# Query and key chunks with their own loads of x and their own dates, in an attention and expert kernel

## The reference

```python
qkv = x @ Wqkv
q, k, v = jnp.split(qkv, 3, axis=-1)
...
for i in range(H):
    ...
    q_rot = _apply_rotary(q[:, i], cos, sin)
    k_rot = _apply_rotary(k[:, i], cos, sin)
    att = jnp.einsum('btd,bsd->bts', q_rot, k_rot) * scale
    if cascade_bias is not None:
        att = att + cascade_w[i - 1] * cascade_bias
    att = jnp.where(causal, -jnp.inf, att)
    att = jax.nn.softmax(att, axis=-1)
    out_i = jnp.einsum('bts,bsd->btd', att, v[:, i])
    head_outputs.append(out_i)
    cascade_bias = jnp.mean(att, axis=1, keepdims=True)
...
x = _layernorm(x + _L0_attn_ref(x, ...), axis=-1)
x = _layernorm(x + _L0_ffn_ref(x, ...), axis=-1)
```

## Time and profile before

| | us |
|---|---|
| median of 3 runs | 3427.57 |
| lowest and highest of them | 3421.42, 3430.92 |
| span of the profiled execution | 3421.5 |
| first exponential of turn 0 | 46.5 |
| first exponential of turns 8, 64, 224, 248 | 163.1, 811.3, 2798.0, 3100.3 |
| mean granted TensorE clock | 0.967 |

### The profile page before, as it was taken

One profiled execution on the slowest core, in us unless ns is written; L12 is line 12 of the kernel. 1 busy time (PEld: TensorE's weight loads), 2 busy tenths in 40 slices (PEclk: granted clock), 3 DMA queues, 4 the chain that ended last, 5 costly groups with the idle time before them and its releaser, 6 DMA issues.

```text
span 3421.5 us, 95130 instructions
## 1 busy us (share of the span) xinstructions
PE 3079.1 (90%) x29668; PEld 1592.4 (47%) x29668; DVE 2747.6 (80%) x9925; ACT 3055.5 (89%) x8882; POOL 2127.2 (62%) x6194
## 2 busy tenths in 40 slices
PE   7898888888999899999999989999999988989855
PEld 3444444443544445554554434555455544544544
DVE  7777777777888788888988897888888987888754
ACT  4999999999989989999999998999999999989634
POOL 6556566564655467876666666777766645666245
PEclk8999999999999999999999999999999999999976
DMA  5322223223334324444433423444334433444354
GB/s 164 94 79 87 85 59 87 76 73 90 93 101 111 104 84 120 120 123 131 128 111 112 123 64 110 116 120 145 104 111 117 125 83 100 130 118 136 97 185 126
DMA packets 270810, 371.12 MB, mean 108 GB/s; under 512 B 61669, under 2 KB 177389, under 8 KB 270304
## 3 DMA queue, kind: packets, MB, share of 16 engines
q1 hardware_dynamic: 255056, 326.65, 33.2%
q0 software_dynamic: 14976, 37.34, 3.8%
q10 hardware_dynamic: 272, 1.05, 0.1%
HBM read 260.02 MB, written 104.40 MB: 107 GB/s over the span
## 4 chain that ended last, share of the span: by engine, by line
PE 36%; DVE 8%; issue 7%; ACT 5%; POOL 4%; SPq 2%; DMA 1%; another core or an unknown queue 1%; POOLq 0%; DVEq 0%; ACTq 0%
PE pv L1240 8%; PE scores L1209 7%; PE scores L1222 6%; DVE att_a L1527 4%; PE side L1369 3%; PE side L1269 2%; ACT att_t L1406 2%; ACT att_a L1396 2%; PE side L1295 2%; PE side L1376 1%; PE scores L1224 1%; PE side L1283 1%; PE scores L1369 1%; SPq L2028 1%
## 5 line engine op out<-in xcount | busy, mean ns | idle before, releaser
L1396 ACT ACTIVATE att_a<-att_a,neg_max 128x128 f32<-128x128 f32 (+7 forms) x2048 | 1609.8, 786 | 52.5 <-DVE neg_max L1527 48.7
L1406 ACT ACTIVATE att_t<-scores 128x1024 f32<-128x1024 f32 (+7 forms) x2048 | 1343.0, 656 | 68.7 <-PE scores L1224 53.7
L1527 DVE CUSTOM_DVE_ANT_0 att_a<-scores,window 128x512 f32<-128x512 f32 (+3 forms) x2048 | 1146.8, 585 | 240.2 <-PE scores L1209 133.7
L1209 PE MATMUL scores<-k_stack,q_stack 99*128 99x512 bf16 (+3 forms) x3072 | 919.0, 335 | 132.6 <-DVE neg_max L1527 112.1
L1240 PE MATMUL pv<-att_t,v_sb 128*32 128x256 f32 (+7 forms) x16384 | 898.8, 299 | 1.9 <-ACT att_t L1406 1.7
L1222 PE MATMUL scores<-q_stack,k_stack 104*128 104x512 bf16 (+3 forms) x3072 | 842.7, 332 | 62.8 <-ACT att_t L1406 50.2
L1527 DVE CUSTOM_DVE_ANT_0 att_a<-scores,window,neg_max 128x512 f32<-128x512 f32 (+3 forms) x1024 | 557.8, 545 | 110.4 <-PE scores L1209 92.9
L1209 PEld LDWEIGHTS scores<-k_stack,q_stack 99*128 99x128 bf16 x3072 | 280.1, 98 | 572.8 <-DVE neg_max L1527 345.6
L1240 PEld LDWEIGHTS pv<-att_t,v_sb 128*32 128x32 f32 x16384 | 340.0, 108 | 413.0 <-issue 334.1
L1222 PEld LDWEIGHTS scores<-q_stack,k_stack 104*128 104x128 bf16 x3072 | 275.3, 98 | 402.4 <-issue 197.9
L1224 PE MATMUL scores<-identb,mask 128*128 128x128 bf16 x2048 | 451.9, 222 | 0.0
(11 more groups left out here) (307 smaller groups left out, 4367.5 us busy)
## 6 DMA issues: line engine op xcount, KB each, us to landing
runner_r<-in_experts SPq DMA_DIRECT2D x137, 384.0 KB
qk_parts<-of_proj SPq DMA_DIRECT2D x128, 384.0 KB
of_proj<-in_xt SPq DMA_DIRECT2D x29, 1024.0 KB
q_stack<-qk_parts SPq DMA_DIRECT2D x256, 96.0 KB
k_stack<-qk_parts SPq DMA_DIRECT2D x256, 96.0 KB
q_stack<-qk_parts SPq DMA_DIRECT2D x256, 64.0 KB
k_stack<-qk_parts SPq DMA_DIRECT2D x256, 64.0 KB
head_out<-o_sb SPq DMA_DIRECT2D x252, 64.0 KB
```

The source lines that it names most:

```text
L1209: engine.matmul(piece_room(c), qs[0:ROWS_A, i * P:(i + 1) * P], ks[0:ROWS_A, low:high], start=True, stop=True).then_inc(s_a_filled, 1)
L1396: engine.activation(taken, taken, EXP, scale=-1.0, bias=neg_max[:, n, i:i + 1], accum_out=row_sum[:, n, i:i + 1]).then_inc(s_exp_a, 1)
L1406: engine.activation(att_t[:, ring:ring + end - base], scores[:, base:end], EXP, accum_out=col_sum[:, n, j:j + 1]).then_inc(s_exp_b, 1)
L1527: engine.tensor_tensor_reduce(out=att_a[:, ring + low:ring + high], in0=piece_room(c), in1=window[:, T - A_LONG[p] + low:T - A_LONG[p] + h ...
```

## The change

Chunks get loads of their own, and so do values from m = 4 on: 60 loads of x instead of 32, listed in LOADS with their room. The chunks of rounds 1 to 3 begin evenly over turns 3 to 63, about five turns an m; those of rounds 4 to 7 over turns 64 to 223, ten turns an m, in four of them one each. The value jobs begin where they did. The gate product goes with the chunks. Until m = 11 the values' x lies in runner_r, all other x in of_proj. A load is put into play four turns before the job that wants it. g_keep now also waits in the plan for the readers of the routing logits two groups back, and the first tile's gather for the last reader of runner_r.

```diff
-    def x_room(m):
-        return (m % 2, m // 2 + 1) if m < SLOTS else (0, m - 1)
-    def x_before(m):
-        return m - 2 if m <= SLOTS else m - 1
     FIRST = 4 * SLOTS
+    AHEAD = 3
+    BEHIND = 3
+    def qk_turn_of(m):
+        k = m - SLOTS
+        if k < AHEAD * SLOTS:
+            return BEHIND + k * (2 * SPAN - BEHIND) // (AHEAD * SLOTS)
+        k -= AHEAD * SLOTS
+        return 2 * SPAN + k * (ROUNDS - 3) * SPAN // ((ROUNDS - 1 - AHEAD) * SLOTS)
+    def chunk_turn(n):
+        m, c = divmod(n, 4)
+        return qk_turn_of(m) + (c if m < (AHEAD + 1) * SLOTS else (0, 1, 3, 4)[c])
+    def value_turn(n):
+        m, c = divmod(n, 2)
+        r, slot = divmod(m, SLOTS)
+        return (r - 1) * SPAN + (BEHIND if r == 1 else 0) + 7 * slot + 4 + c
+    def has_room(m):
+        return m < 3 * SLOTS
+    LOADS = [(m % 2, m, "both", 0) for m in range(SLOTS)]
+    LOADS += sorted([(0, m, "qk", qk_turn_of(m)) for m in range(SLOTS, ROUNDS * SLOTS)] +
+                    [(1 if has_room(m) else 0, m, "v", value_turn(2 * m)) for m in range(SLOTS, ROUNDS * SLOTS)],
+                    key=lambda load: (load[3], load[2], load[1]))
+    LOAD_OF = {(what, m): i for i, (_, m, whats, _) in enumerate(LOADS)
+               for what in (("qk", "v") if whats == "both" else (whats,))}
+    def x_room(i):
+        return LOADS[i][0], len([k for k in range(i + 1) if LOADS[k][0] == LOADS[i][0]])
+    def x_before(i):
+        was = [k for k in range(i) if LOADS[k][0] == LOADS[i][0]]
+        return was[-1] if was else None
...
-        return [Stage("g_x", m, hold=1.5, after=(("x_load", m), ("w_center", 0))), Stage("g_turn", m, frees=True), Stage("g_keep", m)]
+        return [Stage("g_x", m, hold=1.5, after=(("x_load", LOAD_OF["qk", m]), ("w_center", 0))), Stage("g_turn", m, frees=True),
+                Stage("g_keep", m, after=tuple(("f_logit", (m // SLOTS // KT - 2) * QUADS + q) for q in range(QUADS)))]
...
-        def x_stage(m):
-            was = x_before(m)
-            gated = (("g_x", was),) if was >= 0 and with_gate(was) else ()
-            return Stage("x_load", m, after=(("v_b", 2 * was + 1), ("qk_b", 4 * was + 3)) + gated if was >= 0 else ())
+        def x_stage(i):
+            was = x_before(i)
+            if was is None:
+                return Stage("x_load", i)
+            _, m, whats, _ = LOADS[was]
+            free = (("v_b", 2 * m + 1),) if whats != "qk" else ()
+            if whats != "v":
+                free += (("qk_b", 4 * m + 3),) + ((("g_x", m),) if with_gate(m) else ())
+            return Stage("x_load", i, after=free)
...
-                if x_ == BEHIND:
-                    project(1, 0)
-                if in_round == 28 and r + 2 < ROUNDS:
-                    project(r + 2, 0)
-                if r + 1 < ROUNDS:
-                    slot, piece = divmod(in_round - (BEHIND if r == 0 else 0), 7)
-                    if 0 <= slot < SLOTS:
-                        m = (r + 1) * SLOTS + slot
-                        if piece == 6 and slot + 1 < SLOTS:
-                            project(r + 1, slot + 1)
-                        if piece < 4:
-                            begin(chunk_job(4 * m + piece), 0)
-                        elif piece < 6:
-                            begin(value_job(2 * m + piece - 4), 0)
-                        if piece == 5 and with_gate(m):
-                            begin(gate_job(m), 0)
+                for i, (_, m, _, wanted) in enumerate(LOADS):
+                    if m >= SLOTS and max(BEHIND, wanted - 4) == x_:
+                        project(i)
+                for n in range(FIRST, 4 * SLOTS * ROUNDS):
+                    if chunk_turn(n) == x_:
+                        begin(chunk_job(n), 0)
+                        if n % 4 == 3 and with_gate(n // 4):
+                            begin(gate_job(n // 4), 0)
+                for n in range(2 * SLOTS, 2 * SLOTS * ROUNDS):
+                    if value_turn(n) == x_:
+                        begin(value_job(n), 0)
...
-            r, slot = divmod(n, SLOTS)
+            r, slot = divmod(LOADS[n][1], SLOTS)
             k, was = x_room(n)[0], x_before(n)
-            if was >= 0:
-                line.wait_ge(s["v_b"], nth["v_b", 2 * was + 1])
-                line.wait_ge(s["qk_b"], nth["qk_b", 4 * was + 3])
-                if with_gate(was):
-                    line.wait_ge(s["g_x"], nth["g_x", was])
+            if was is not None:
+                _, m, whats, _ = LOADS[was]
+                if whats != "qk":
+                    line.wait_ge(s["v_b"], nth["v_b", 2 * m + 1])
+                if whats != "v":
+                    line.wait_ge(s["qk_b"], nth["qk_b", 4 * m + 3])
+                    if with_gate(m):
+                        line.wait_ge(s["g_x"], nth["g_x", m])
...
+                        if n == (0, 0):
+                            last = max(m for room, m, whats, _ in LOADS if room == 1)
+                            pool.wait_ge(s["v_b"], nth["v_b", 2 * last + 1])
```

More of the change, by code:

```diff
@@ L800, in turn @@
                     for slot in range(SLOTS):
[L801 removed]
+                        project(slot)
                         if slot == 0:
@@ L1268, in tensor_program @@
                         col = c // 2 * C + half * P
-                        made = engine.matmul(room, w_qkv[:, k, col:col + P], xT[x_room(m)[0]][:, k, c % 2 * WB:(c % 2 + 1) * WB],
+                        made = engine.matmul(room, w_qkv[:, k, col:col + P], xT[x_room(load)[0]][:, k, c % 2 * WB:(c % 2 + 1) * WB],
                                              start=(k == 0), stop=(k == KT - 1))
@@ L1282, in tensor_program @@
                                 t0 = (4 * quad + j) * P
-                                made = engine.matmul(room[:, j * P:(j + 1) * P], xT[x_room(m)[0]][:, k, t0:t0 + P],
+                                made = engine.matmul(room[:, j * P:(j + 1) * P], xT[x_room(load)[0]][:, k, t0:t0 + P],
                                                      w_qkv[:, k, col:col + P], start=(k == 0), stop=(k == KT - 1))
```

29 lines of the change are left out of this document (15 added, 14 removed).

## The result

The changed kernel takes 3456.8 us (median of 4; 3452.9 to 3462.7), the kernel before beside it 3428.5: a ratio of 1.0087, 95% interval 1.0071 to 1.0104. It is slower by 28 us where 8 us faster was forecast, and outside the range of 3395 to 3444. The late stage, at 2007 us on the profile, lies beyond every case of the prediction: the highest of them had it at 1983.

A forecast was written before the change was run, and what follows sets the result against it. ScalarE was taken to end last in turns 8 to 63, with stalls behind TensorE and VectorE side work later. Terms -13, +7, +2 and -4 for the clock gave -8 us from 3427.6: 3420 us, range 3395 to 3444.

The forecast's parts named there:

- the highest of them: Rival for turns 64 to 223: other jobs fill the freed places, nothing happens; late stage 1983 us, total 3430; chance 0.16.
- The late stage, dates (-13): Turns 64 to 223: sixteen chunks and four gate products leave, each us of TensorE side work worth 0.35 us; -13 us.
- upper bound of 39.7: Turns 64 to 223: all TensorE time of the sixteen chunks and four gate products comes back, 39.7 us.
- The -4 for fewer falls of the clock: Turns 64 to 223: less work may mean fewer falls of TensorE's clock; a tenth of 40 us lost, -4 us.
- The loads (+2): 28 more 1 MB loads of x: a late landing at every fourth of fifteen tight places; +2 us, at most 26.
- case 2: Rival: from turn 64 value products wait for their load in the one x room; +30 us, about 3450; chance 0.14.
- The first 64 turns (+7, up to 22): Denser chunks there: four more groups cost 3.8 us, meetings with values 3; +7 us, between 0 and 22.
- case 3: Rival: the first 64 turns pay all the later ones win, chunks 15 us and collisions 8; 3440 us; chance 0.14.
- TensorE near 11 us a turn: Sign for turns 8 to 63: TensorE busy near 11 us a turn, the stage taking 648 + 7 us.

The follow-up runs named there:

- chip B: Not a run but a kind of chip: the one on which the kernel before takes 3356 to 3359 us.
- chip A: Not a run but a kind of chip: the one on which the kernel before takes 3420 to 3432 us; the first result is from it.
- old dates: The changed kernel with its separate loads, rooms and gates, but every chunk begun at its turn in the kernel before; ratio to the kernel before 1.0065.
- copies: The kernel before with 28 added 1 MB copies from HBM to HBM, each behind a load of x, order unchanged; ratio to the kernel before 1.0036.
- the run with OVERDUE changed: The kernel before with a waiting side job forced in after 8.5 us of the plan's time, not 8.0; ratio to the kernel before 1.0031.
- thin runs: Three runs of the changed kernel, one engine's operations on the first 64 turns' chunks cut to 64 columns; ratios 0.9988 (GpSimd), 1.0010 (TensorE products), 0.9976 (VectorE).
- two rounds: The changed kernel with two rounds of chunks in the first 64 turns instead of three, and five behind; ratio to the kernel before 1.0008.
- the run with chunk 24 moved away: The changed kernel with two rounds ahead, gates begun with the second value job, and x chunk 24's chunks at turn 163, not 159; ratio to the kernel before 1.0011.
- thin run on VectorE: The changed kernel with VectorE's four operations on each of the first 64 turns' 48 chunks cut from 512 to 64 columns; ratio to the kernel before 0.9976.

## Why the prediction was wrong

**The late stage, dates (-13): right in kind, and on a chip B at least as large.** The sixteen chunks and four gates left, and with the loads already separate that took 28 us off the late stage by the traces (1993.7 to 1966.1), or some 19 if the first of them is taken at its median. This is between the forecast and the upper bound of 39.7. The -4 for fewer falls of the clock was wrong: the granted clock of the late stage stayed at 0.98, and its time at half clock went from 61 us to 79 on A.

**The loads (+2): mis-sized, the step that failed most.** I asked only whether a load lands in time, and there I was right: 1.2 us of waits for in_xt, not the 30 us of case 2. What the separation costs is elsewhere: 22 us by the ratio at the old dates, of which the traces put 6 in the first stage and the rest in the late one. It is not in waits for any DMA, which are no longer than before. What the trace does show is a VectorE busy 24 us more than with copies, and a wait for the row minimum of 46.0 us for 33 to 35. I took the separation as loads alone, but it also deals a new order, with sooner gates; by the run with OVERDUE changed some 10 of the 22 us may be a draw. Why this order costs what it does stays open. The 12 us of the copies do not explain it, since their waits for other DMAs are missing here.

**The first 64 turns (+7, up to 22): inside its bounds, mis-sized.** It was 11 to 16, above my forecast and below case 3's +23. TensorE near 11 us a turn was right (10.9). I priced the fourth chunk of a group and the meetings with values, and nothing for two things. One is the fall of the clock: the earlier trace rows showed 1.00 there, and I took it as given; the half clock costs an estimated 7 us, as worked out above. The other is that VectorE and GpSimd serve four chunks in five turns in one chain with TensorE: each of the thin runs gives time back. In the stage ScalarE is busy 4.7 us more, and its waits for TensorE's second product and the row minimum rise from 4.9 to 16.9 us: together the 16.

**The meeting with the routing: not in the sum.** I wrote that another order deals the stalls anew, and widened each case by 10 us. One such event alone was worth 18 us on A and 11 on B, by the ratios of the runs that moved chunk 25. That it stands there could be read from the order: the routing's steps from turn 153 and the products of x chunk 25 in turns 155 to 158. Its price could not. The old order has a meeting too: chunk 24's products run in turns 160 to 163, the routing's from 159 to 165, and turns 160 to 167 take 109.8 us. With two rounds such a meeting costs nothing that is seen, and the run with chunk 24 moved away did not beat the kernel before.

**What chip A adds.** 18 us of the 30 are not seen on B. On A both kernels show waits of VectorE and ScalarE without a releaser in the profile. In the late stage they sum to 20, 28, 16 and 24 us in the four traces of the kernel before, to 35 and 42 in two of the changed one, and to none in any of the eleven traces from B. By the means, 38 less 22, they account for up to 16 of the 24 us by which the late stage's difference is larger on A (+21 for -3); the two engines' waits partly lie on top of each other. But they are not all that sets A apart: the run with chunk 24 moved has only 10 us of them in its late stage, and that stage takes 32 us more than nearly the same order on B. Why the changed kernel has more of them, and what else A adds, is open.

**In sum, on B:** by the traces, first stage +6 for separate loads and gates and +10 for the dates; late stage +25 and -28. By the ratios, +21.8 for the preparation and -9.4 for the dates, together the +12.4 measured. The prediction had +2 for the loads and -10 for the dates in both stages (+7, -13 and -4).

## What to carry to other kernels

Price what a move needs (its loads, its buffers, its changed partners) by itself before pricing the move: here the preparation alone cost 0.65%, and the move only won it back in part. A stage in which one engine is busy 98% and the others far less is not free room: each us of side work cut on a partner of its chain came back as 0.1 to 0.3 us. Compare stage times only with how far each trace lies from the median in mind. And look where a one-off job, as the routing, falls in the new order.

## What the runs showed of the hardware

**VectorE reading SBUF beside GpSimd.** Line 1613, which reads two tiles of SBUF, in turns 8 to 63, in the changed kernel on B and in the run with GpSimd's chunk operations cut to 64 columns (min/median/max in ns); line 1810 of the changed kernel, which reads two tiles as well; and line 1623, a cast of one tile, in the same two runs as line 1613 (busy us, mean ns):

```profile
L1613 DVE SCALAR_TENSOR_TENSOR of_proj<-of_proj x45: 677/692/1764, 163.5 to 809.5; 128x512 f32<-128x512 f32 x45
L1613 DVE SCALAR_TENSOR_TENSOR of_proj<-of_proj x45: 677/686/807, 164.2 to 789.8; 128x512 f32<-128x512 f32 x45
L1810 DVE TENSOR_TENSOR row_hot<-iota,in_tile x32: 682/686/1755, 1163.7 to 3305.7; 128x512 bf16<-128x512 bf16 x32
L1623 DVE CAST of_proj<-of_proj 128x512 bf16<-128x512 f32 x45 | 31.9, 709 | 0.6
L1623 DVE CAST of_proj<-of_proj 128x512 bf16<-128x512 f32 x45 | 19.5, 434 | 0.6
```

Line 1613's mean falls from 968 to 710 ns, its longest case from 1764 to 807, and line 1623's mean from 709 to 434 ns when GpSimd works less beside them; the row minimum, which reads one input from PSUM, keeps 586 and 587 ns as a mean. Line 1810's 1.75 us fell in the routing (turn 156), beside GpSimd's line 1988, with TensorE waiting 1.4 us behind it. The Trainium skill ("GPSIMD Engine Reference", 8. Key points) says that GpSimd shares its SBUF interfaces with VectorE and contends with its instructions of two SBUF inputs or in what it calls a 2-port perf mode; the rows of lines 1613 and 1810 agree, and in which mode line 1623 runs no trace shows. I had added nothing for it. In the stage the two lines cost VectorE 12 us each, which at the 0.33 of the thin run on VectorE is an estimated 8 us.

**The same copy on two chips.** VectorE's copy of a tile (line 1854) behind the transposes that feed it, first on A, then on B, TensorE's row ahead of VectorE's:

```profile
2036.16 0.66 PE L1396 MATMUL side<-ident,runner_r 128*128 128x128 f32 x4
2040.26 0.76 DVE L1854 COPY runner_r<-side 128x256 f32<-128x256 f32 x2 [4.33 <-remote]
2020.45 0.66 PE L1396 MATMUL side<-ident,runner_r 128*128 128x128 f32 x4
2020.93 0.76 DVE L1854 COPY runner_r<-side 128x256 f32<-128x256 f32 x2 [0.70 <-issue]
```

On B the copy starts 0.5 us after the transposes begin, on A 4.1 us after, with nothing in the profile that it waited for. No such wait stands before 1200 us of the span; the experts' jobs begin at turn 95.
